# A decoder layer on one core: joined weighted sums in the attention, and between it and the experts a bias added by GpSimd, an early query spectrum, rows in halves and filler for the clock

## The reference

```python
x = _layernorm(x + _L0_attn_ref(x, w_qkv, w_out, b_out))
x = _layernorm(x + _L0_xattn_ref(x, ctx_1024, ctx_1024, Wq, bq, Wout, bout))
x = _layernorm(x + _L0_ffn_ref(x, Wg, bg, W1, b1, W2, b2, gamma, beta))
# attention: 16 heads of 8, rotary, softmax(q k^T / sqrt(8)) v
# cross attention:
q = (Q @ Wq + bq).transpose(0, 2, 1)          # 8 channels; k_, v alike from the context
corr = jnp.real(jnp.fft.ifft(jnp.fft.fft(q) * jnp.conj(jnp.fft.fft(k_)))).mean(axis=(0, 1))
W_topk, I_topk = jax.lax.top_k(corr, 11)      # 11 lags for the whole batch
R = sum(w * jnp.roll(v, -shift, axis=-1) for w, shift in zip(softmax(W_topk), I_topk))
out = repeat(R, 16 heads) @ Wout + bout
# experts: 8, ReLU, 256 hidden, top 2 of 8 by logits, softmax of the two; then a layer norm with gamma, beta
```

## Time and profile before

| | us |
|---|---|
| median of 3 runs (250.78 to 252.87) | 252.7 |
| profiled execution, whole | 254.5 |
| its span, first to last instruction | 252.3 |
| TensorE busy in the span | 228.8 (91%) |
| VectorE busy | 187.7 (74%) |
| ScalarE busy | 133.2 (53%) |
| GpSimd busy | 103.7 (41%) |
| attention loop, 9 turns written as `range(7, 16)` | about 30 to 77 |
| seam | about 106 to 131 |

### The profile page before, as it was taken

One profiled execution on the slowest core, in us unless ns is written; L12 is line 12 of the kernel. 1 busy time (PEld: TensorE's weight loads), 2 busy tenths in 40 slices (PEclk: granted clock), 3 DMA queues, 4 the chain that ended last, 5 costly groups with the idle time before them and its releaser, 6 DMA issues.

```text
span 252.3 us, 7126 instructions
## 1 busy us (share of the span) xinstructions
PE 228.8 (91%) x2696; PEld 185.6 (74%) x2696; DVE 187.7 (74%) x629; ACT 133.2 (53%) x220; POOL 103.7 (41%) x213
## 2 busy tenths in 40 slices
PE   7999899999999868599899999999999999999930
PEld 6777677777777646435657899789987899789920
DVE  0688998889989994724525568896799778864884
ACT  2688889989999944320238700494028700691000
POOL 4287876998889970320050300053001600120323
PEclk9999999999999999956999999999999999999995
DMA  6912447454465522100000000001000100001001
GB/s 153 292 42 52 66 57 125 98 124 102 114 138 125 105 60 70 26 0 0 1 3 0 0 0 3 1 0 44 0 4 0 42 3 1 0 0 44 0 12 31
DMA packets 32307, 12.22 MB, mean 48 GB/s; under 512 B 19889, under 2 KB 32146, under 8 KB 32274
## 3 DMA queue, kind: packets, MB, share of 16 engines
q1 hardware_dynamic: 31554, 11.48, 20.9%
q10 hardware_dynamic: 720, 0.30, 0.6%
HBM read 6.26 MB, written 1.05 MB: 29 GB/s over the span
## 4 chain that ended last, share of the span: by engine, by line
PE 65%; DVE 23%; issue 6%; ACT 3%; POOL 1%; DVEq 0%; POOLq 0%
PE scoreT_pair L1118 9%; PE bank L1132 7%; PE score_pair L1118 6%; PE bank L895 6%; PE scoreT_pair L1132 6%; PE bank L899 5%; PE bank L820 4%; DVE x_ext L1497 4%; PE bank L801 3%; PE bank L858 3%; PE score_pair L836 3%; DVE rowmax L1183 2%; PE scoreT_pair L852 2%; DVE odd_sum L1497 2%; PE bank L912 2%
## 5 line engine op out<-in xcount | busy, mean ns | idle before, releaser
L552 POOL TENSOR_TENSOR ve<-mv,table 128x4 f32<-128x4 f32 (+1 forms) x18 | 4.4, 246 | 109.1 <-DVE mv L1509 71.6
L1183 DVE TENSOR_REDUCE rowmax<-score_pair 128x8 f32<-128x1024 f32 x32 | 38.9, 1215 | 3.2 <-PE score_pair L836 2.8
L654 ACT ACTIVATE early<-scoreT_pair 128x1024 f32<-128x1024 f32 x32 | 32.6, 1019 | 5.2 <-PE scoreT_pair L852 5.1
L1132 PE MATMUL bank<-w,early 128*128 128x128 f32 x256 | 30.1, 276 | 0.0
L1132 PE MATMUL scoreT_pair<-w,early 128*128 128x128 f32 x256 | 29.9, 275 | 0.0
L1132 PEld LDWEIGHTS bank<-w,early 128*128 128x128 f32 x256 | 29.5, 192 | 0.4
L1132 PEld LDWEIGHTS scoreT_pair<-w,early 128*128 128x128 f32 x256 | 29.2, 192 | 0.0
L1118 PE MATMUL scoreT_pair<-x2T_part,w_part 128*128 128x512 f32 x96 | 26.2, 403 | 1.1 <-DVE odd_sum L1497 1.1
L895 PE MATMUL bank<-early,v_pad 128*32 128x128 f32 x512 | 26.4, 278 | 0.0
L899 PE MATMUL bank<-early,head_ones 128*32 128x128 f32 x512 | 25.7, 273 | 0.0
L1118 PE MATMUL score_pair<-x2T_part,w_part 128*128 128x512 f32 x96 | 25.6, 400 | 0.0
(11 more groups left out here) (185 smaller groups left out, 463.4 us busy)
## 6 DMA issues: line engine op xcount, KB each, us to landing
w<-in_w SPq DMA_DIRECT2D x8, 256.0 KB, 3.1
x_ext<-in_x SPq DMA_DIRECT2D x4, 256.0 KB, 5.4
qT_all<-mT SPq DMA_DIRECT2D x32, 32.0 KB, 2.3
early<-in_xT SPq DMA_DIRECT2D x3, 256.0 KB, 4.5
early<-in_ctxT SPq DMA_DIRECT2D x3, 256.0 KB, 4.9
out<-qkv_all SPq DMA_DIRECT2D x3, 256.0 KB, 2.4
table<-in_tables SPq DMA_DIRECT2D x1, 321.0 KB, 3.5
out<-qkv_all SPq DMA_DIRECT2D x4, 64.0 KB, 1.5
```

The lines of the kernel that those rows point to most:

```text
L654: act.activation(prob[n % 2][:, 2 * u:2 * u + 2, :, :], scoreT_pair[:, :].rearrange("p (i j s) -> p i j s", i=2, j=QUAD), ACT.Exp, scale=S ...
L1132: mm = pe.matmul(expert_bank[k % 4][:, e4 * D:(e4 + 1) * D], hT[:, f, n * P:(n + 1) * P], w2[:, f, :], start=(c == 0), stop=(c == CH - 1))
L1183: dve.tensor_reduce(rowmax[:, H // 2 * u:H // 2 * (u + 1)], score_pair[:, :].rearrange("p (r t) -> p r t", t=S), AX_X, ALU.max).then_inc(s ...
```

## The change

It has five parts.

1. *Order of the attention.* All engines' lists are rewritten. In a turn TensorE now does both weighted sums of a row side by side, and a group of `scoresT` next to a group of `scores` twice. The loop runs from 8 to 15. Filler at the start goes from 20 to 13 products of 128 columns.
2. *Cross bias.* `start_cross_out` is gone; `add_cross_bias(g)` on GpSimd adds `bout` (sent to all partitions by a transfer) to the rows `x1b` of each group. Group 0 is done when all rows are there, the others once the lag weights are ready.
3. *Query spectrum.* It is made from `x1_all` directly, 13 rows ahead of the last projection and 3 behind it; the bias comes in as one product that touches only frequency 0. `cross_queries` is gone.
4. *First group in halves.* Sums, statistics, deviations, rows, transposes and the split in parts are done for two rows and two rows. The first expert products need only the high part.
5. *Filler.* `stay_busy` with 512 columns becomes `keep_clock` with 128 columns, in other counts. Ahead of the choice of lags, the maximum is taken from PSUM, before the copy.

The diff, cut to its core:

```diff
+Q_AHEAD = 13
+HALF = GT // 2
...
-                    sp.dma_start(bout_row[:, :], a["bout"].unsqueeze(0)).then_inc(s["bout_in"], 16)
+                    sp.dma_start(bias[:, CROSS_OUT, :], a["bout"].partition_broadcast(P)).then_inc(s["bout_in"], 16)
+                    sp.dma_start(bq_row[:, :], a["bq"].unsqueeze(0)).then_inc(s["late_tables"], 16)
...
+            for k in range(8, 16):
+                rope_sum(pool, k - 1)
+                third_piece(pool, k - 2)
+                small_columns(k - 4)
+                inverse_deviation(k - 8)
+                remainder(pool, k - 1)
+                rope_products(pool, k)
+                pad_v(k - 4)
...
             third_piece(pool, 15)
-            inverse_deviation(7)
-            inverse_deviation(8)
-            pad_v(12)
+            pad_v(13)
             w1_low_piece(0)
             w1_low_piece(1)
             w1_low_piece(2)
+            inverse_deviation(8)
             w1_low_piece(3)
...
+            def add_cross_bias(g):
+                if g == 0:
+                    pool.wait_ge(s["bout_in"], 16)
+                    pool.wait_ge(s["x1_ready"], B)
+                else:
+                    pool.wait_ge(s["circ_ready"], 1)
+                pool.tensor_tensor(x1b[:, g, :, :], x1b[:, g, :, :], bias[:, CROSS_OUT, :].unsqueeze(1).broadcast_to([P, GT, D]),
+                                   ALU.add).then_inc(s["x1b_ready"], 1)
...
+                if g == 0:
+                    for half in range(2):
+                        tiles = slice(HALF * half, HALF * (half + 1))
+                        rsqrt(half, tiles.stop, tiles, "y2_aggr", mv2, ve2, "ve2_ready", rs2, "rs2_ready")
...
+            for k in range(8, 16):
+                softmax_exp(k - 6, 0)
+                second_piece(k - 2)
                 second_copy(k - 2)
                 softmax_exp(k - 6, 1)
+                kT_copy(k - 3)
+                first_piece(k - 1)
                 keep_qkv(k)
-                first_piece(k - 1)
                 mT_copy(k - 4)
...
+            def start_query_spectrum():
+
+                wait(pe, s["k_T"], B)
+                pe.wait_ge(s["rows_ready"], 2)
+                pe.matmul(turn_bank[0:NF, 0:P], constant_row[:, :], bq_row[:, :].unsqueeze(1).broadcast_to([1, B, XC]), start=True, stop=False,
+                          skip_group_check=True)
+                pe.wait_ge(s["x1_ready"], Q_AHEAD)
...
+            def finish_query_spectrum():
+                pe.wait_ge(s["x1_ready"], B)
...
-            for k in range(7, 16):
-                scoresT(k - 6, 1)
+            for k in range(8, 16):
+                scoresT(k - 6, 0)
+                scores(k - 4, 0)
                 qkv(k)
                 project(k - 7)
+                scoresT(k - 6, 1)
+                scores(k - 4, 1)
                 weighted(k - 6, 0)
-                scores(k - 3, 0)
-                scoresT(k - 5, 0)
-                maxima_transpose(k - 4)
                 weighted(k - 6, 1)
                 k_transposes(k - 2)
-                scores(k - 3, 1)
+                maxima_transpose(k - 4)
...
+            key_spectrum()
+            start_query_spectrum()
             project(15)
-            key_spectrum()
-            for g in range(G):
-                start_cross_out(g)
-            pe.wait_ge(s["q_nat"], 1)
-            spectrum(turn_bank, q_all[:, :, :].rearrange("p b c -> p (b c)"), "q_freq")
-
-            stay_busy(2, ident4)
+            keep_clock(7)
+            finish_query_spectrum()
+
+            keep_clock(7)
...
-            stay_busy(3, ident4)
+            keep_clock(11)
...
-                    for k, (w, x) in enumerate(((0, 0), (0, 1), (1, 0))):
+                    for k, (w, x) in enumerate(((0, 0), (1, 0), (0, 1))):
+                        if c == 0 and x == 1:
+                            pe.wait_ge(s["x2T_low"], g + 2)
...
-            stay_busy(2, ident4)
-            x2_transpose(0)
-            stay_busy(2, ident4)
+            pe.wait_ge(s["x_kept"], 2)
+            keep_clock(4)
+            first_transpose(0)
+            first_transpose(1)
...
+            for k in range(8, 16):
+                maxima(k - 4, 0)
+                if live(k - 9):
+                    normal_rows(dve, k - 9)
+                residual_sum(k - 7)
+                maxima(k - 4, 1)
+                statistics_of_rows(k - 7)
+                pieces_of_maxima(dve, k - 4)
                 reciprocal(k - 6)
                 mean_and_variance(k - 7)
                 divide(k - 6)
...
-            cross_queries()
...
+            dve.max(best[:, 0:8], pv_bank[:, 0:S]).then_inc(s["topk"], 1)
             dve.tensor_copy(corr[:, :], pv_bank[:, 0:S]).then_inc(s["corr_copied"], 1)
             dve.wait_ge(s["corr_copied"], 1)
-            dve.max(best[:, 0:8], corr[:, :]).then_inc(s["topk"], 1)
...
+            first_sums()
+            first_rows()
+            first_rest(0)
+            first_rest(1)
```

397 lines of the change are left out of this document (230 added, 167 removed).

## The result

| | before | after |
|---|---|---|
| median of the runs, us | 251.74 (250.21 to 252.87, 4 runs) | 242.69 (242.13 to 243.11, 4 runs) |
| ratio, with its 95% interval | | 0.9643 (0.9576 to 0.971) |
| span of the profiled execution | 252.3 | 241.2 |

What follows compares the result with a forecast made beforehand. TensorE was taken to set the attention loop, with little needed work between attention and experts. Terms 1.4 + 1.6 + 6.7 + 0.1 + 1.6 = 11.4 us, off the 252.7 median, gave 241.3; range 238.6 to 246.0.

Steps and rivals of the forecast that it cites:

- The loop: Attention loop: fewer changes of the array's split save 0.18 us a turn, 1.4 in eight turns; bounds 0 and 1.9.
- The wait for the exponential: Loop turn: the second weighted half waits about 0.06 us for its exponential, taken off the 0.24 saved on split changes.
- Rival (a): Attention gains nothing, as ScalarE or GpSimd holds the turn at 5.15 us; 244.3 us in all; chance 0.15.
- Start and end of the attention: Start 0.3, maxima copy no longer held 0.9, moved projection 0.4: 1.6 us gained; bounds -1.5 and +3.
- Spectra and correlation: Between attention and experts: VectorE has the correlation at 112.2 instead of 118.90, 6.7 us less; bounds 4.5 and 7.0.
- rival (b): The clock falls to half all the same between attention and experts, about 3.5 us more: 244.8 us; chance 0.10.
- Maximum direct: Choice of the lags: the maximum reads PSUM directly with the copy behind it, so one hand-over goes, 0.1 us.
- First group in halves: First expert product 5.05 us behind the first group's sum instead of 6.66: 1.6 us gained; bounds 0.9 and 2.1.
- Rival (c): First half's rows wait for the second half's power: 0.55 us more, 241.9; inside the forecast, which with it has 0.70.
- The rule weighed against the trace: Skill's rule: two-port VectorE tensor_scalar and GpSimd lock each other out; the first half's rows would wait for the second power.
- The experts: From the first expert product to the end: same work in the same order, 121.5 us as before.
- Rival (d): Slower: TensorE waits a full 1.12 us more for exponentials once per turn, 253.3 us; twice, 262; chance 0.03.

Runs made afterwards that it cites:

- `full_between`: Changed kernel plus one unread whole-array product of 8 columns between the two weighted halves in each of the 8 turns; 246.08 us.
- `no_filler`: Changed kernel without the `keep_clock` products between the last projection and the first transposes of the experts' input; 244.74 us, ratio 0.9631.
- `bias_early`: Changed kernel with GpSimd's cross bias additions to groups 1 to 3 put right behind group 0; 247.75 us, ratio 0.98.
- `order_only`: Kernel before with only the new attention order on all engines, its old stretch between attention and experts kept; 250.68 us, ratio 0.9862.
- `whole_group`: Changed kernel with the first group made in one piece again instead of two halves; 243.4 us, ratio 0.9612.
- `one_row`: Changed kernel with the 7 filler products behind the last projection replaced by four of one row and 512 columns; 245.1 us, ratio 0.9648.

## Why the prediction was right, and where its terms were off

**The loop.** Right in kind and in size: 0.15 a turn instead of 0.18, 1.2 in 8 turns instead of 1.4. The changes of split were sized rightly: by the chains four that cost 0.14, 0.10, 0.10 and 0.14 went and two of 0.10 and 0.14 came, 0.24 less. The wait for the exponential was 0.09 instead of 0.06, which leaves 0.15. `full_between` shows that changes put back cost time, and not less than that. Rival (a) is out.

**Start and end of the attention.** Forecast 1.6, found 2.15 (0.27 and 1.88). In kind: the copy of the maxima isn't held any more (0.24 and 0.17 in the two places at the end). The size is not as firm as it looks. In the traces of kernels with this attention the exponential of row 2 starts anywhere between 33.3 and 35.1, and the projection between 101.9 and 103.9. One part of that is seen: in the first profile of the changed kernel the scores of the last row wait 0.45. By the code they wait for the transfer that turns the row's queries (`q_transpose`, L326). It was issued at 83.08 and landed 4.5 us later, at about 87.6. It took 4.5 in `no_filler` too, and there the same scores wait 0.44; in the ten other traces with this attention it took 3.1 to 3.9, and the scores don't wait. Timeline of the changed kernel, and the last line of its view of L326:

```profile
83.08 1.27 SPq L326 DMA_TRANSPOSE qT_all<-stack  x1
...
87.66 0.40 PE L898 MATMUL score_pair<-kT_all,qT_all 48*128 48x128 bf16 x8 [0.45 <-issue]
DMA to landing us min/median/max: 4.5/4.5/4.5
```

The profile gives no releaser for that wait, but in all twelve traces it goes with the late landing. Why it took longer there is not shown.

**Spectra and correlation.** Forecast 6.7, found 6.35 (5.01 and 1.34). The spectra were nearly right (5.1 forecast, 5.0 found, the lag spectrum 1.81 as before). The term that was off is the correlation: VectorE has it 0.81 behind the lag spectrum, not 0.5, as four pieces take 0.71 even at the full clock. The clock stayed at 1.00, so rival (b) is out, and `no_filler` shows that it would have come true by 2.1 without the filler.

**Maximum direct.** 0.13 for 0.1.

**First group in halves.** 1.60 for 1.6, 5.06 for 5.05 behind the sum. That both agree so well is luck; inside errors cancel. GpSimd was not late by 0.45 but by 0.09: its three additions ended at 115.56, VectorE's statistics of the first half at 115.49. Against that these statistics took 1.47 from the sum, where I had 1.30, and between the last row and the first product lie 0.95, where I had 0.8. The name of the term was wrong as well: only 0.56 come from the halves, 0.7 from the wait for the low part that is gone, and 0.34 from transposes that start row by row behind a shorter filler. The filler ahead of the first product, which the forecast named as a cause, had no part in it. Rival (c) is out: the first rows ran beside the second power. The rule weighed against the trace in the forecast failed for that pair, and came true for another pair in `bias_early`.

**The experts.** Here a step failed that the forecast had as nothing: from the first product to the end 122.1 instead of 121.8 (252.3 - 130.52; the 121.5 that the forecast gives "as before" is not what its rows say). It is in each of the kernels with the new seam (122.0 to 122.3) and not in `order_only` (121.8), so it is no noise. 0.23 of it is one wait of TensorE at the start of group 1, 0.59 instead of 0.36, for VectorE, which ahead of it pauses 0.44 instead of 0.23 between two instructions on the gates. `whole_group` and `one_row`, with fewer and with more instructions in VectorE's list ahead of that place, lack this pause, but their end is no nearer (122.3 and 122.1). What the pause waits for, and where the rest of the 0.3 lies, stays open.

**The sum.** 11.4 forecast, 11.1 found in the span. Rival (d) had no part in it. By the medians it is less, 9.05 and 10.4. The forecast took a sum that was read from an execution of 254.5 us off a median of 252.7. Taken off its own execution it gives 243.1, and the profiled execution of the changed kernel took 242.94. No trace was taken of the kernel before where its mean clock was 0.977, so how much smaller the seam's gain is there stays open.

## What to carry to other kernels

Where TensorE is the bound, count the changes of its split in a turn, and put pieces of the same split side by side as far as their operands are there; each change cost 0.10 to 0.14 us in this loop. In a serial stretch, keep the clock with short products over all rows that end before the next operand comes, as length is what they can cost. Before an idle engine is given work, see what the other one does beside it: 3.7 us of GpSimd's additions cost 5.5 where they met three short instructions of VectorE, and at most 0.09 five microseconds later.

## What the runs showed of the chip

- Under products of one row the clock fell from 2.4 to 1.2 GHz within 2 us, with TensorE busy throughout (`one_row`, the one execution that was traced); before the change the clock fell at 108 under such products too.
- Beside a run of GpSimd's additions each of three VectorE instructions lasted about as long as one addition (1.24): 1.29, 1.30 and 1.36 for 0.28, 0.28 and 0.34. The product of the spectra, with one operand in PSUM, kept its 0.42 beside them.
- Such a hold can cost more than its length: 3.05 on VectorE became 5.5, since the clock fell in the gap.
- The same attention ends at places up to 2 us apart in different traces, while the stretch behind it repeats to a hundredth (15.91 in both traces of the changed kernel). A difference of less than 1% is best read from landmarks within the trace.
